# Separate instruction orders, a diagonal skip product and an own bank for the output product in the last 24 steps of a fused Mamba-style block and FP4 feed-forward

## Chip, core and metric

The kernel runs on one core of a Trainium2 chip. The metric is the device time of one execution in microseconds, the median of several runs.

## What is computed

The reference is one layer: a simplified state-space block and a feed-forward with blockwise FP4 rounding, each followed by a residual sum and layer norm. x is 8 x 2048 x 256 float32.

```python
xz = x @ W_in;  x_proj, z = split(xz)                  # 256 -> 2 x 512
x_conv = silu(causal_conv4(x_proj) + conv_b)
ssm = x_conv @ W_xproj                                 # 33 columns: delta, B (16), C (16)
delta = softplus(ssm[..., 0])
h_mean = einsum('bld,bln->bdn', x_conv, delta[..., None] * Bm) / L
y = einsum('bdn,bln->bld', h_mean, Cm)
y = (y + D * x_conv) * silu(z)
x1 = layernorm(x + y @ W_out)
gate, up = fp4_linear(x1, w_gate), fp4_linear(x1, w_up)   # 256 -> 704
out = layernorm(x1 + fp4_linear(silu(gate) * up, w_down)) # 704 -> 256
```

fp4_linear rounds both operands in groups of 16 along the contraction: absolute maximum, scale, division, rounding to the grid, product with the scale.

## The kernel before

Rows of x are worked in 32 groups of 512 rows (NSUP = 32), each group in four steps (j = 0 to 3), so a step is a quarter group. The first half, phase 1, makes x_conv and silu(z) of a group, writes both to HBM, and adds the group's share to the state h_mean, which is whole only when all four groups of a batch are through. The second half, phase 2, runs LAG = 5 groups later: it reads x_conv and silu(z) back (xl and zl, in the tile early), makes y, the output product, layer norm and the feed-forward for 128 rows per step. The loop `walk` therefore goes over g_ = 0 to 38. Each step works on seven different tiles at once, at different stages: u and v (phase 1), w (y, skip, gate), to (output product, attention sum, layer norm), tx (rounding of x), tg (gate and up product, rounding of h), td (down product), tz (FFN sum, second layer norm). Phase 1 ends with g_ = 31; its last pieces lie in g_ = 32. So for g_ = 33 to 38, the last 24 steps, only the later stages are left: y, skip and gate in the first 16 of them, everything but these in the next four, and the drain in the last four.

The order of work is written out by hand on each engine, as the body of `walk`, and semaphores tie them together. Each engine runs its queue in order, so that a wait holds everything behind it. In a late step:

- PE (TensorE): gate and up product into pgu (L518, 18 matmuls), six transposes of h into pe_ and pb (L558), y product into pc (L569, 48 rows deep, 512 columns), output product into pd (L580, four full-precision matmuls of 256 columns), two transposes of x into pe_ (L630), down product into pd (L518, 17 matmuls). Output and down product share the bank pd: down waits for the attention sum of the same step to have read it (r_done), the output product for the FFN sum (r2_done). State products (L591, 512 columns, full precision) belong to phase 1.
- DVE (VectorE): FFN sum (L1089), absmax (L908), scale (L911), inverse (L914), divide (L918, here "codes") and the two rounding steps (L924, L927) of x; h product (L1114); skip, xl times D plus pc, into g (L1033); absmax of h (L908), two subtractions that make the low parts of the transposed h, "rests" (L1123, L1126), h scale and inverse (L911, L914), attention sum (L1140), h codes (L918), rests of x (L1152), the two rounding steps of h (L924, L927). The scaled values are written before rounding; ScalarE makes 2^22 times their magnitude in between (L841 for x, L879 for h), and rounding waits for it.
- ACT (ScalarE): squared deviations (L755), magnitude of x (L841), SiLU of the gate (L845), high parts of the transposed h (L853, L856), output rows (L864), high part of the transposed x (L873), magnitude of h (L879), rows of the first layer norm (L890).
- POOL (GpSimd): layer norms (L404, L406, L408, one element a partition), product of x with its scale (L429), gate: g times zl (L446), product of h with its scale (L456, L458).
- SP (SyncE): all transfers, in the same step order: next xres, next xl and zl (after g_ready), the store of the finished tile (after out_ready).

## Time and profile before

| what | value |
|---|---|
| median of 3 runs | 2015.34 us (2013.84 to 2023.07) |
| profiled execution, its own time | 2014.19 us |
| its span, first to last instruction | 2012.3 us |
| PE busy | 1920.6 us, 95% |
| DVE busy | 1708.1 us, 85% |
| ACT busy | 1280.9 us, 64% |
| POOL busy | 1081.0 us, 54% |
| mean granted TensorE clock | 0.981 of full speed |
| chain that ended last | PE 83%, DVE 7%, issue 5%, ACT 3%, POOL 2% |

Busy time of an engine is the union of its instructions. The granted clock is a share of 2.4 GHz; 0.5 would be 1.2 GHz throughout. Starts are microseconds from the first instruction. A matmul's end is modelled, so times of TensorE are best read from one start to the next; the same holds for VectorE, where an instruction's row overlaps the next by a little. A full-precision matmul is written in two records.

### The profile page before, as it was taken

The page shows a single profiled execution, that of the slowest core. Times are in us where ns is not written, and L with a number is a line of the kernel's source. Part 1 is how long each engine was busy: PE and PEld are TensorE (multiplying, and loading weights), DVE is VectorE, ACT ScalarE, POOL GpSimd, SP SyncE. Part 2 cuts the span into 40 slices and gives each one's busy share as a digit, 9 for nine tenths or more (in the row PEclk, how much of TensorE's full clock was granted, in tenths as well). Part 3 has the DMA queues.
Part 4 walks back from the last instruction along what each step waited for, and adds up shares of the span by engine and source line. Part 5 has one row for each costly group of instructions (what it writes and reads, how often), then busy time and mean ns, then how long its engine had stood idle before and what let it go on. Part 6 is the DMA issues. An engine that isn't in the chain of part 4 may idle for free.

```text
span 2012.3 us, 33985 instructions
## 1 busy us (share of the span) xinstructions
PE 1920.6 (95%) x10148; PEld 1541.0 (77%) x10148; DVE 1708.1 (85%) x3293; ACT 1280.9 (64%) x2613; POOL 1081.0 (54%) x1774
## 2 busy tenths in 40 slices
PE   6898999999999999999999999999999999888886
PEld 5666788888888888878887888888887887666665
DVE  6655889988988898999888989988889898887886
ACT  6776666666766666666666666766666675444443
POOL 3534555555555555555555555555555555544543
PEclk8898999999999999999999999999999999989999
DMA  5234232323232232323232232323222322221200
GB/s 169 91 127 141 90 105 98 102 91 110 97 104 99 94 106 87 108 98 108 98 104 99 85 105 98 112 93 108 97 91 102 106 89 85 64 63 64 63 24 14
DMA packets 120307, 190.58 MB, mean 95 GB/s; under 512 B 15040, under 2 KB 49728, under 8 KB 120128
## 3 DMA queue, kind: packets, MB, share of 16 engines
q1 hardware_dynamic: 120128, 188.42, 28.0%
q8 instruction: 85, 1.39, 0.3%
q14 instruction: 94, 0.77, 0.1%
HBM read 104.48 MB, written 83.89 MB: 94 GB/s over the span
## 4 chain that ended last, share of the span: by engine, by line
PE 83%; DVE 7%; issue 5%; ACT 3%; POOL 2%; SPq 0%; DMA 0%; POOLq 0%; DVEq 0%; ACTq 0%
PE pgu L518 23%; PE pd L518 13%; PE pd L580 10%; PE pb L518 8%; PE pa L518 8%; PE pc L591 5%; PE pc L607 5%; PE pa L620 2%; PE pe_ L558 2%; PE pc L569 2%; PE pe_ L630 1%; DVE acc L1009 1%; PE pb L558 1%; DVE qsh L908 1%; DVE g L1033 1%
## 5 line engine op out<-in xcount | busy, mean ns | idle before, releaser
L518 PE MATMUL pgu<-wgu_hi,xqT 128*128 128x512 f32 (+1 forms) x1536 | 428.4, 387 | 1.0 <-ACT xqT L873 1.0
L518 PE MATMUL pd<-wd_hi,hqT 128*128 128x256 f32 (+1 forms) x1536 | 323.0, 302 | 21.7 <-DVE scratch L1140 17.4
L518 PEld LDWEIGHTS pgu<-wgu_hi,xqT 128*128 128x128 f32 x1536 | 279.3, 190 | 65.1 <-issue 2.0
L518 PEld LDWEIGHTS pd<-wd_hi,hqT 128*128 128x128 f32 (+1 forms) x1536 | 253.6, 195 | 49.9 <-issue 30.1
L580 PE MATMUL pd<-wout,g 128*128 128x256 f32 x1024 | 254.8, 392 | 0.0
L404 POOL TENSOR_SCALAR rs<-ssq 128x1 f32<-128x1 f32 x256 | 51.1, 200 | 379.0 <-issue 364.2
L924 DVE SCALAR_TENSOR_TENSOR scratch<-scratch 128x256 f32<-128x256 f32 (+2 forms) x258 | 171.2, 664 | 71.4 <-ACT scratch L879 57.9
L518 PE MATMUL pgu<-wgu_lo,xqT 128*128 128x512 f32 (+1 forms) x768 | 227.2, 377 | 0.0
L755 ACT ACTIVATE scratch<-scratch,sum 128x256 f32<-128x256 f32 x256 | 129.9, 507 | 152.6 <-DVE scratch L1089 134.7
L1009 DVE SCALAR_TENSOR_TENSOR acc<-xps,cw,acc 128x512 f32<-128x512 f32 x256 | 202.2, 790 | 28.7 <-POOL acc L438 24.0
L580 PEld LDWEIGHTS pd<-wout,g 128*128 128x128 f32 x1024 | 184.0, 189 | 49.7 <-issue 29.8
L446 POOL TENSOR_TENSOR g<-g,early 128x512 f32<-128x512 f32 x128 | 163.6, 1278 | 48.6 <-DVE g L1033 48.3
L458 POOL TENSOR_TENSOR scratch<-hnq,qsh 128x704 f32<-128x704 bf16 x128 | 188.8, 1475 | 0.0
L518 PE MATMUL pd<-wd_lo,hqT 128*128 128x256 f32 x640 | 184.9, 289 | 0.0
L408 POOL TENSOR_SCALAR nm<-sum,rs 128x1 f32<-128x1 f32 x256 | 152.5, 596 | 44.0 <-POOL rs L406 44.0
L438 POOL TENSOR_TENSOR acc<-acc,tap 128x512 f32<-128x512 f32 x128 | 164.2, 1283 | 11.4 <-ACT tap L799 11.4
L406 POOL TENSOR_TENSOR rs<-rs,nhalf 128x1 f32<-128x1 f32 x256 | 151.7, 592 | 21.6
L607 PEld LDWEIGHTS pc<-wxp,xcs 128*128 128x128 f32 x1024 | 134.1, 194 | 37.6 <-ACT xcs L782 20.6
L518 PEld LDWEIGHTS pgu<-wgu_lo,xqT 128*128 128x128 f32 x768 | 144.4, 190 | 23.3
L429 POOL TENSOR_TENSOR scratch<-xnq,qsx 128x256 f32<-128x256 bf16 x128 | 81.3, 635 | 130.2 <-DVE xnq L927 129.7
L607 PE MATMUL pc<-wxp,xcs 128*128 128x33 f32 x1024 | 128.3, 270 | 23.6 <-ACT xcs L782 16.5
L873 ACT ACTIVATE xqT<-pe_ 128x256 fp32r<-128x256 f32 x128 | 48.7, 381 | 152.7 <-PE pe_ L630 152.7
(130 smaller groups left out, 4542.9 us busy)
## 6 DMA issues: line engine op xcount, KB each, us to landing
sz_hbm<-szs SPq DMA_DIRECT2D x128, 256.0 KB, 2.0
xc_hbm<-xcs SPq DMA_DIRECT2D x128, 256.0 KB, 2.0
early<-xc_hbm SPq DMA_DIRECT2D x128, 256.0 KB, 2.7
early<-sz_hbm SPq DMA_DIRECT2D x128, 256.0 KB, 3.0
xin<-in_x_t_dram SPq DMA_DIRECT2D x32, 512.0 KB, 4.7
xres<-in_L_attn_x_dram SPq DMA_DIRECT2D x128, 128.0 KB, 2.4
out_dram<-scratch SPq DMA_DIRECT2D x128, 128.0 KB, 1.7
early<-in_L_attn_W_in_dram SPq DMA_DIRECT2D x2, 512.0 KB, 4.7
```

Of the source, the lines that this page charges most:

```text
L406: pool.tensor_tensor(rs[:, :], rs[:, :], nhalf[:, :], ALU.pow).then_inc(rs_done, 1)
L408: pool.tensor_scalar(nm[:, :], total[:, :], rs[:, :], -1.0 / DM, ALU.mult, ALU.mult)\
L438: pool.tensor_tensor(acc[:, j % 2, :], acc[:, j % 2, :], tap0[:, j % 2, :], ALU.add).then_inc(tap_done, 1)
L446: pool.tensor_tensor(g[:, second(s) % 2, j, :], g[:, second(s) % 2, j, :], zl[:, j % 2, :], ALU.mult).then_inc(g_ready, 1)
L458: pool.tensor_tensor(blocks(hq[:, 0:FF]), blocks(hnq[:, :]), spread(qsh[:, :, 1]), ALU.mult).then_inc(hprod_done, 1)
L518: mm = pe.matmul(bank, lhsT, rhs, start=(m == 0), stop=(m == len(pairs) - 1))
L580: mm = pe.matmul(pd[:, 0:DM], g[:, (second(s) + 1) % 2, c, j * P:(j + 1) * P], wout[:, c, :], start=(c == 0), stop=(c == NB - 1))
L591: mm = pe.matmul(pc[0:H3, :], dB[:, t, :], xct[:, (n - 1) % 2, t, :], start=(t == 0), stop=(t == TPS - 1))
L607: mm = pe.matmul(pc[:, t * NX:(t + 1) * NX], xcs[:, jb % 2, t * P:(t + 1) * P], wxp[:, jb, :], start=True, stop=True)
L755: act.activation(dev[:, :], r, ACT.Square, bias=total[:, :], scale=-1.0 * DM, accum_out=ssq[:, :]).then_inc(ssq_done, 1)
L924: return dve.scalar_tensor_tensor(v, big, HALF_STEP, v, ALU.max, ALU.add)
L1009: dve.scalar_tensor_tensor(acc[:, jb % 2, :], xps[:, jb % 2, k:k + ST], cw[:, jb, k:k + 1], acc[:, jb % 2, :], ALU.mult, ALU.add).then_inc ...
```

## The change

It touches only steps with g_ > NSUP, the last 24, and the preparation of one table in the group before.

- Skip: where VectorE computed xl * D + pc, TensorE now adds diag(D) times xl into the bank pc behind the y product (`skip_product`). The four diagonal matrices, `diag`, are made by ScalarE in step j = 2 of g_ = 32.
- Gate: VectorE multiplies pc by zl straight into g (`gated`); POOL's gate is left out, and the y product waits for the gate of the tile before in place of the skip.
- Output product: it goes to the bank pa, free of phase 1 by then (`out_bank`). It waits for the attention sum of the tile before, and the down product for the FFN sum of the tile before, no longer for this step's attention sum.
- The two layer norms get a deviation buffer each (`dev`).
- Orders: each engine has its own list for these steps. The other added functions (ffn_sum, x_codes, h_product and so on) hold the old statements unchanged, so that both lists can call them.

```diff
+        diag = sb("diag", [P, NB, P])
...
-        dev = over_scratch(DM)
+        dev = over_scratch(2 * DM).rearrange("p (n d) -> p n d", n=2)
...
+        def out_bank(g_):
+            return pa if g_ > NSUP else pd
...
+                    def x_values():
+                        pool.wait_ge(xq_link, 6 * tx + 6)
+                        at_least(pool, xq_pe, tx)
+                        pool.tensor_tensor(blocks(xv[:, :]), blocks(xnq[:, :]), spread(qsx[:, :, 1]),
+                                           ALU.mult).then_inc(xprod_done, 1)
+                    if exists(tx) and g_ > NSUP:
+                        x_values()
                     if exists(tz):
                         layer_norm(tz, ssq2_done, out_ready, rs2_eps, rs2_done, nm2_done, sum2, ssq2, rs2, nm2)
...
+                    if exists(to) and g_ > NSUP:
+                        layer_norm(to, ssq1_done, r1_ready, rs1_eps, rs1_done, nm1_done, sum1, ssq1, rs1, nm1)
+                    if p2 and g_ <= NSUP:
...
-                    if exists(to):
+                    if exists(to) and g_ <= NSUP:
...
-                wait_apart(pe, (h_ready, b - 1 if s == 0 else b), (ct_ready, g_ - LAG + 1), (yd_done, w),
+                wait_apart(pe, (h_ready, b - 1 if s == 0 else b), (ct_ready, g_ - LAG + 1), (g_ready if g_ > NSUP else yd_done, w),
                            (ssm_added, capped(v, NT)))
                 if j == 3 and g_ == LAG:
                     pe.wait_ge(h_added, g_)
-                pe.matmul(pc[:, :], hcat[:, j * P:(j + 1) * P], ctr[:, second(s), :], start=True, stop=True)\
-                    .then_inc(y_pe, 1)
-            def output_projection(j, s, i, tz):
+                mm = pe.matmul(pc[:, :], hcat[:, j * P:(j + 1) * P], ctr[:, second(s), :], start=True,
+                               stop=g_ <= NSUP)
+                if g_ <= NSUP:
+                    mm.then_inc(y_pe, 1)
+            def skip_product(j, i, w):
+                pe.wait_ge(xl_landed[j % 2], 16 * (2 * i + j // 2 + 1))
+                if w == 4 * (NSUP - LAG + 1):
+                    pe.wait_ge(diag_ready, NB)
+                pe.matmul(pc[:, :], diag[:, j, :], xl[:, j % 2, :], start=False, stop=True).then_inc(y_pe, 1)
+            def output_projection(j, s, i, g_, to, tz):
                 pe.wait_ge(g_ready, 4 * i)
-                at_least(pe, r2_done, capped(tz + 1, NT))
+                if g_ > NSUP:
+                    pe.wait_ge(ct_ready, NSUP)
+                    pe.wait_ge(r_done, to)
+                else:
+                    at_least(pe, r2_done, capped(tz + 1, NT))
+                bank = out_bank(g_)
                 if i == 1 and j == 0:
                     pe.wait_ge(w_landed, 32)
                     pe.wait_ge(ct_ready, LAG)
                 for c in range(NB):
-                    mm = pe.matmul(pd[:, 0:DM], g[:, (second(s) + 1) % 2, c, j * P:(j + 1) * P],
+                    mm = pe.matmul(bank[:, 0:DM], g[:, (second(s) + 1) % 2, c, j * P:(j + 1) * P],
                                    wout[:, c, :], start=(c == 0), stop=(c == NB - 1))
...
-            def down_projection(to, td):
+            def down_projection(g_, to, td):
                 pe.wait_ge(hqT_hi, 2 * td + 2)
                 pe.wait_ge(hqT_lo, 2 * td + 2)
-                pe.wait_ge(r_done, capped(to + 1, NT))
+                if g_ > NSUP:
+                    pe.wait_ge(r2_done, td)
+                else:
+                    pe.wait_ge(r_done, capped(to + 1, NT))
                 pairs = []
                 for c in range(FC):
                     pairs += [(hqT[:, c, :], wd_hi[:, c, :]),
...
+                    if g_ > NSUP:
+                        if exists(tg):
+                            gate_and_up(tg)
+                        if p2:
+                            y_product(j, s, b, g_, v, w)
+                        if exists(td):
+                            transposed_h(td, u)
+                        if exists(to):
+                            output_projection(j, s, i, g_, to, tz)
+                        if p2:
+                            skip_product(j, i, w)
+                        if exists(tx):
+                            transposed_x(td, tx)
+                        if exists(td):
+                            down_projection(g_, to, td)
+                        continue
...
-                act.activation(dev[:, :], r, ACT.Square, bias=total[:, :], scale=-1.0 * DM,
+                act.activation(dev[:, 0 if ssq is ssq1 else 1, :], r, ACT.Square, bias=total[:, :], scale=-1.0 * DM,
...
+                    if g_ > NSUP:
+                        if exists(tg):
+                            gate_silu()
+                        if exists(tx):
+                            x_big()
+                        if exists(td):
+                            h_highs()
+                        if exists(tz):
+                            deviations(r2_done, tz, r2[:, :], sum2, ssq2, ssq2_done)
+                        if exists(tx):
+                            x_highs()
+                        if exists(to):
+                            deviations(r_done, to, r1[:, j, :], sum1, ssq1, ssq1_done)
+                        if exists(tg):
+                            h_magnitude()
+                        if exists(to):
+                            r1_rows()
+                        if exists(tz):
+                            out_rows()
+                        continue
...
+                    if g_ == NSUP and j == 2:
+                        act.wait_ge(w_landed, 32)
+                        for c in range(NB):
+                            act.activation(diag[:, c, :], ident[:, :], ACT.Copy, scale=dsk[:, c:c + 1])\
+                                .then_inc(diag_ready, 1)
...
+                        dve.scalar_tensor_tensor(r1[:, j, :], out_bank(g_)[:, 0:DM], 1.0, xres[:, j % 2, :], ALU.mult, ALU.add,
+                                                 accum_out=sum1[:, :]).then_inc(r_done, 1)
...
+                    def gated():
+                        if w == 4 * (NSUP - LAG + 1):
+                            dve.wait_ge(g_ready, w)
+                        dve.wait_ge(y_pe, w + 1)
+                        dve.wait_ge(zl_landed[j % 2], 16 * (2 * i + j // 2 + 1))
+                        at_least(dve, o_pe, 4 * i - 4)
+                        dve.tensor_tensor(g[:, second(s) % 2, j, :], pc[:, :], zl[:, j % 2, :],
+                                          ALU.mult).then_inc(g_ready, 1)
+                    if g_ > NSUP:
+                        if exists(tz):
+                            ffn_sum()
+                        if exists(tx):
+                            x_codes()
+                        if exists(tg):
+                            h_product()
+                        if exists(tx):
+                            x_round()
+                        if exists(td):
+                            h_rests()
+                        if exists(tg):
+                            h_absmax()
+                        if exists(to):
+                            attn_sum()
+                        if exists(tg):
+                            h_scales()
+                            h_codes()
+                        if exists(tx):
+                            x_rests()
+                        if exists(tg):
+                            h_round()
+                        if p2:
+                            gated()
+                        continue
```

TensorE's queue, one step of the 16, from the end of the gate and up product to the start of the down product. Before:

```order
L518 MATMUL pgu<-wgu_hi,xqT 128x384 x2
L558 MATMUL pe_<-ident,scratch 128x128 x4
L558 MATMUL pb<-ident,scratch 128x128 x2
L569 MATMUL pc<-ctr,hcat 128x512
L580 MATMUL pd<-wout,g 128x256 x4
L630 MATMUL pe_<-ident,scratch 128x128 x2
L518 MATMUL pd<-wd_hi,hqT 128x256
```

After:

```order
L531 MATMUL pgu<-wgu_hi,xqT 128x384 x2
L582 MATMUL pc<-ctr,hcat 128x512
L571 MATMUL pe_<-ident,scratch 128x128 x4
L571 MATMUL pb<-ident,scratch 128x128 x2
L607 MATMUL pa<-wout,g 128x256 x4
L592 MATMUL pc<-early,diag 128x512
L657 MATMUL pe_<-ident,scratch 128x128 x2
L531 MATMUL pd<-wd_hi,hqT 128x256
```

The y product has moved ahead of the transposes, the output product writes pa, and a 512-column product of early (xl) and diag stands between it and the transposes of x.

VectorE's queue, one step of the 16, from the rounding of x and the h product on. Before:

```order
L924 SCALAR_TENSOR_TENSOR scratch<-scratch 128x256
L927 SCALAR_TENSOR_TENSOR xnq<-scratch 128x256
L1114 TENSOR_TENSOR scratch<-scratch,pgu 128x704
L1033 SCALAR_TENSOR_TENSOR g<-early,dsk,pc 128x512
L908 TENSOR_REDUCE qsh<-scratch 128x44
L1123 TENSOR_TENSOR hqT<-pe_,hqT 128x512
L1126 TENSOR_TENSOR hqT<-pb,hqT 128x256
L911 TENSOR_SCALAR qsh<-qsh 128x44
L914 RECIPROCAL qsh<-qsh 128x44
L1140 SCALAR_TENSOR_TENSOR scratch,sum1<-pd,xres 128x256
L918 SCALAR_TENSOR_TENSOR scratch<-scratch,qsh 128x704
```

After:

```order
L1187 TENSOR_TENSOR scratch<-scratch,pgu 128x704
L1016 SCALAR_TENSOR_TENSOR scratch<-scratch 128x256
L1019 SCALAR_TENSOR_TENSOR xnq<-scratch 128x256
L1196 TENSOR_TENSOR hqT<-pe_,hqT 128x512
L1199 TENSOR_TENSOR hqT<-pb,hqT 128x256
L1000 TENSOR_REDUCE qsh<-scratch 128x44
L1215 SCALAR_TENSOR_TENSOR scratch,sum1<-pa,xres 128x256
L1003 TENSOR_SCALAR qsh<-qsh 128x44
L1006 RECIPROCAL qsh<-qsh 128x44
L1010 SCALAR_TENSOR_TENSOR scratch<-scratch,qsh 128x704
L1225 TENSOR_TENSOR xqT<-pe_,xqT 128x256
```

The rounding of x (its first step L924 before, L1016 after) has moved behind the h product, the rests before the absmax of h, the attention sum before the h scale, and the skip is gone from this place.

VectorE's queue at the seam of two such steps, from the x rests over the h rounding. Before:

```order
L1152 TENSOR_TENSOR xqT<-pe_,xqT 128x256
L924 SCALAR_TENSOR_TENSOR scratch<-scratch 128x704
L927 SCALAR_TENSOR_TENSOR hnq<-scratch 128x704
L1089 SCALAR_TENSOR_TENSOR scratch,sum2<-pd,scratch 128x256
L908 TENSOR_REDUCE qsx<-scratch 128x16
```

After:

```order
L1225 TENSOR_TENSOR xqT<-pe_,xqT 128x256
L1016 SCALAR_TENSOR_TENSOR scratch<-scratch 128x704
L1019 SCALAR_TENSOR_TENSOR hnq<-scratch 128x704
L1242 TENSOR_TENSOR g<-pc,early 128x512
L1161 SCALAR_TENSOR_TENSOR scratch,sum2<-pd,scratch 128x256
```

The gate, g from pc and early (zl), now stands between the last rounding of h and the FFN sum.

## Rows read from the trace of the kernel before

**Rows 1.** Stretches: us, busy (count) of PE PEld DVE ACT POOL, clock, DMA, GB/s

```profile
1731.23:1930.42 199.19, 171.33 (x834) 137.54 (x833) 162.59 (x341) 86.99 (x193) 100.68 (x162) 0.92 0.19 60
1930.42:1976.42 46.00, 38.93 (x206) 32.27 (x205) 37.02 (x79) 21.02 (x47) 19.40 (x36) 0.95 0.06 18
1856.83:1869.91 13.08, 11.40 (x53) 9.32 (x53) 11.09 (x23) 6.00 (x13) 6.78 (x13) 0.87 0.26 84
1894.55:1906.12 11.57, 9.89 (x53) 7.91 (x52) 10.15 (x22) 5.41 (x12) 6.22 (x11) 1.00 0.21 68
```

**Rows 2.** Timeline, one step at clock 1.00: start, us, engine, line, operation [idle before]

```profile
1895.49 0.42 DVE L1089 SCALAR_TENSOR_TENSOR scratch<-pd,scratch 128x256 f32<-128x256 f32 x1
...
1895.91 1.43 POOL L458 TENSOR_TENSOR scratch<-hnq,qsh 128x704 f32<-128x704 bf16 x1
...
1896.35 1.02 DVE L911 TENSOR_SCALAR qsx<-qsx 128x16 f32<-128x16 f32 x1
...
1897.76 0.42 DVE L918 SCALAR_TENSOR_TENSOR scratch<-scratch,qsx 128x256 f32<-128x256 f32 x1
...
1898.67 0.42 DVE L924 SCALAR_TENSOR_TENSOR scratch<-scratch 128x256 f32<-128x256 f32 x1 [0.48 <-ACT scratch L841]
1898.69 0.76 ACT L845 ACTIVATE scratch<-pgu 128x704 f32<-128x704 f32 x1
...
1899.48 0.89 DVE L1114 TENSOR_TENSOR scratch<-scratch,pgu 128x704 f32<-128x704 f32 x1
...
1900.29 0.74 DVE L1033 SCALAR_TENSOR_TENSOR g<-early,dsk,pc 128x512 f32<-128x512 f32 x1
...
1900.95 0.88 DVE L908 TENSOR_REDUCE qsh<-scratch 128x44 f32<-128x704 f32 x1
...
1901.74 0.68 DVE L1123 TENSOR_TENSOR hqT<-pe_,hqT 128x512 fp32r<-128x512 f32 x1
...
1902.57 0.41 PE L630 MATMUL pe_<-ident,scratch 128*128 128x128 f32 x2 [0.90 <-DVE hqT L1123]
1902.67 0.18 DVE L911 TENSOR_SCALAR qsh<-qsh 128x44 f32<-128x44 f32 x1
...
1903.52 0.88 DVE L918 SCALAR_TENSOR_TENSOR scratch<-scratch,qsh 128x704 f32<-128x704 f32 x1
...
1903.75 0.36 PE L518 MATMUL pd<-wd_hi,hqT 128*128 128x256 f32 x1 [0.77 <-DVE scratch L1140]
...
1904.33 0.42 DVE L1152 TENSOR_TENSOR xqT<-pe_,xqT 128x256 fp32r<-128x256 f32 x1
...
1905.27 0.89 DVE L924 SCALAR_TENSOR_TENSOR scratch<-scratch 128x704 f32<-128x704 f32 x1 [0.52 <-ACT scratch L879]
...
1907.07 0.42 DVE L1089 SCALAR_TENSOR_TENSOR scratch<-pd,scratch 128x256 f32<-128x256 f32 x1
```

**Rows 3.** Timeline of TensorE alone, a phase 1 and 2 step without idle time

```profile
1592.27 0.73 PE L518 MATMUL pgu<-wgu_hi,xqT 128*128 128x512 f32 x2
...
1596.22 0.62 PE L518 MATMUL pa<-xt_hi,win_hi 128*128 128x512 f32 x2
...
1597.61 0.60 PE L558 MATMUL pe_<-ident,scratch 128*128 128x128 f32 x4
...
1598.78 1.99 PE L580 MATMUL pd<-wout,g 128*128 128x256 f32 x8
1600.70 3.63 PE L591 MATMUL pc<-xct,dB 128*48 128x512 f32 x8
1604.27 0.44 PE L630 MATMUL pe_<-ident,scratch 128*128 128x128 f32 x2
1604.46 0.71 PE L518 MATMUL pb<-xt_hi,win_hi 128*128 128x512 f32 x2
...
1607.13 0.37 PE L518 MATMUL pd<-wd_hi,hqT 128*128 128x256 f32 x1
...
1609.52 0.73 PE L518 MATMUL pgu<-wgu_hi,xqT 128*128 128x512 f32 x2
```

More of the change, by code:

```diff
@@ new lines, in x_highs, with h_magnitude @@
+                    def x_highs():
+                        act.wait_ge(xq_pe, tx + 1)
+                        act.activation(xqT[:, 0:KM, :], pe_[:, 0:DM].rearrange("p (c n) -> p c n", c=KM), ACT.Copy)\
+                            .then_inc(xqT_hi, 1)
+                    def h_magnitude():
+                        act.wait_ge(hq_link, 6 * tg + 4)
+                        act.activation(hbuf[:, 0:FF], hbuf[:, FF:2 * FF], ACT.Abs, scale=TWO22)\
+                            .then_inc(hbig_ready, 1)
@@ new lines, in r1_rows @@
+                    def r1_rows():
+                        act.wait_ge(nm1_done, to + 1)
+                        act.activation(r1[:, j, :], r1[:, j, :], ACT.Identity, bias=nm1[:, :], scale=rs1[:, :])\
+                            .then_inc(r1_ready, 1)
+                    if g_ > NSUP:
[18 more added lines that the diff above has]
+                        continue
@@ L877, in body @@
                     if exists(tg):
[L878 to L880 removed]
+                        h_magnitude()
                     if p1 and td >= 0:
@@ L1063, in mean_state, with ffn_sum, x_codes @@
                         dve.wait_ge(h_link, 2 * b)
+                    def ffn_sum():
+                        dve.wait_ge(dn_pe, tz + 1)
+                        at_least(dve, out_ready, tz)
+                        dve.scalar_tensor_tensor(r2[:, :], pd[:, 0:DM], 1.0, r1[:, j, :], ALU.mult, ALU.add,
+                                                 accum_out=sum2[:, :]).then_inc(r2_done, 1)
+                    def x_codes():
+                        x_ = r1[:, (j - 1) % TPS, :]
+                        wait_apart(dve, (r1_ready, tx + 1))
+                        q_absmax(x_, small_x).then_inc(xq_link, 1)
+                        at_least(dve, xprod_done, tx)
+                        dve.wait_ge(xq_link, 6 * tx + 1)
+                        q_scale(small_x).then_inc(xq_link, 1)
+                        dve.wait_ge(xq_link, 6 * tx + 2)
+                        q_inverse(small_x).then_inc(xq_link, 1)
+                        at_least(dve, xq_pe, tx)
+                        dve.wait_ge(xq_link, 6 * tx + 3)
+                        q_divide(x_, small_x, xv[:, :]).then_inc(xq_link, 1)
```

165 lines of the change are left out of this document (83 added, 82 removed).

## Prediction

> **What bounds the kernel now.** I read the page first (TensorE is busy nearly everywhere, so most of the program is bound by it), then the stretches that the change covers, then one step of them in order of time on all engines, and last a stretch in which TensorE never waits, for its prices.
>
> The changed steps begin with the gate product at 1731.23 us. Steps 1 to 16 of them (y product still alive) take 199.19 us, 12.45 each, and the next four 46.00 us, 11.50 each [rows 1]. The last four end at the span's end, 2012.3. TensorE is busy for 171.33 of the 199.19, so 14% of that stretch is lost to waiting; its granted clock is 0.92 there, and it is 1.00 in one step and 0.87 in another [rows 1]. A step at clock 1.00 takes 11.57 us, one at 0.87 takes 13.08 [rows 1]. So 12.45 consists of 11.57 of order and 0.88 of lower clock. The lower level (1.2 GHz in place of 2.4) comes after steps in which TensorE stood idle before the transposed x and again before the down product; in the step shown the idle time is 0.90 us on the transposed x and 0.77 on the first down matmul [rows 2].
>
> What makes 11.57? VectorE's own queue, read start to start [rows 2]. From the h product (1899.48): product 0.81, skip 0.66, absmax 0.79, both rests 0.93, scale, inverse and attention sum together 0.85, codes to first rounding 1.75 (this holds the x rests and the wait for ScalarE's magnitude), both roundings 1.80. Then, with the rows of the step's head (1895.49 on), FFN sum and x absmax 0.86, x scale and inverse 1.41, x divide to x rounding 0.91, x rounding 0.81. The sum is 11.58 against 11.57: VectorE has no free time except two waits for ScalarE of about 0.5 us. One of these pieces is strange: the x scale, 16 elements wide, takes 1.02 us, the h scale, 44 wide, takes 0.18. The long one ends at 1897.37, when POOL's 704-wide product ends (1895.91 + 1.43 = 1897.34) [rows 2]. It waited for POOL.
>
> **What TensorE costs when it never waits** [rows 3], start to start: gate and up 3.95, six transposes and the y product 1.17, output product 1.92, four state products of 512 columns in full precision 3.57, so 0.89 each, transposed x 0.19, down 2.39.
>
> **The change part by part.**
> 1. Skip product on TensorE, 16 of them. No row shows it. It moves 512 full-precision columns, as a state product does: 0.89. From below the bound is a cheaper kind of matmul: the y product also has 512 columns and is less than half of the 1.17, so 0.4 at most; from above it is twice a 256-column output matmul, 2 x 1.92/4 = 0.96. I take 0.89, since size and type are equal. A step on TensorE is then 3.95 + 1.17 + 1.92 + 0.89 + 0.19 + 2.39 = **10.51**.
> 2. Gate on VectorE in place of skip. A product of a PSUM and an SBUF operand of 512 columns is what the first rest is; both rests (768 columns) take 0.93, so 0.62. The old skip, also 512 from PSUM, takes 0.66. From above: POOL's price for a product, 1.43 us for 704 columns, gives 1.04. I take 0.66. POOL loses its gate, which no one then waits for; I count nothing.
> 3. VectorE's new order. Leaving out what is equal: the x rounding now stands behind the h product, and ScalarE does the magnitude of x behind the gate's SiLU. That wait is gone: divide to next is then some 0.36, as its own 256-wide work costs elsewhere in this queue (FFN sum and absmax, two such pieces, 0.86), not 0.91. The gate lies between the last h rounding and the FFN sum, so the x scale starts 0.66 later against POOL's product, and waits some 0.2 to 0.35 us, not 0.84. Loop: 0.81 + 0.81 + 0.93 + 0.79 + 0.85 + 1.75 + 1.80 + 0.66 + 0.86 + 0.92 (scale and inverse, 1.41 less 0.49) + 0.36 = **10.5**; 10.3 if the scale waits least. On the rule: the Trainium skill, "SBUF — State Buffer", section "Who interferes with whom", says that VectorE and GpSimd share one port pair as an exclusive lock, taken by an instruction with two SBUF inputs or in a two-port mode. The trace agrees in the 1.02 us row above. By that rule the gate, with one input in PSUM, is not held by POOL, but the h codes and first rounding can be, by the layer-norm chain: that is the second rival.
> 4. TensorE's new order and bank. The output product writes its own bank, so the down product no longer waits for this step's attention sum (0.77 us before it [rows 2]), and the transposed x stands behind output and skip product. Laid out from the gate product's start with the prices above: y 3.95, transposes 4.4, output 5.1, skip 7.0, transposed x 7.9, down 8.1, next gate 10.5. What they wait for: the h product starts 4.93 after the gate (1894.55 to 1899.48; SiLU from 1898.69 [rows 2]); x rounding 5.7 to 6.5; POOL's x product is a third of its 1.43, done by 7.2, before 7.9; rests done by 7.5; x rests at 4.93 + 0.81 + 0.81 + 0.93 + 0.79 + 0.85 + 0.81 + 0.42 = 10.35. The next gate product needs them, 0.16 before TensorE is free. h rounding ends at 12.7, POOL's product at 14.5, and the next step's transposes want it at 10.5 + 4.4 = 14.9. The y product waits for the gate of the step before, done at 13.4, and wants it at 14.5. Every wait is covered, by 0.15 to 1.1 us, so the period is TensorE's.
> 5. ScalarE moves its row outputs last, so SyncE stores a tile and sends the next loads later, but at the latest when the gate of the step before is done, 13.4 - 10.5 = 2.9 us into a step. The skip product needs them in the step after, over 8 us on. Nothing.
> 6. Four scaled copies (the diagonals) on ScalarE in the step group before. ScalarE is busy 86.99 of 199.19 us, 5.4 us a step; 704 columns cost it 0.76 [rows 1, 2], so four of 128 cost under 3 us, in a gap. Nothing, 1 to 3 us if the cover failed.
>
> With TensorE full, its clock should stay up: in the stretch of rows 3 steps of this kind follow each other without idle time. I add 0.1 us for small collisions: **10.6** a step. The next four steps have no y, skip and gate: TensorE needs 10.51 less 0.89 and 0.4, 9.2, but the next gate still waits for the x rests, 10.35; I take 10.45. The last four steps gain nothing: there the chain gate, SiLU, product, codes, POOL, transposes, down is the same in both orders.
>
> **Sum.** 16 x (12.45 - 10.6) = 29.6; 4 x (11.50 - 10.45) = 4.2; less 0.8 for the change of order. Gain 33. The profiled execution took 2014.19 us by its own time (span 2012.3), giving 1981.2; the median of the runs, 2015.34, lies 1.15 above it, giving **1982**. With the low price of the skip product and everything else ideal 10.35 a step, gain 38, 1977; with the high prices 11.0, gain 27, 1988.
>
> **The rivals.**
> A. The lower clock stays. Gaps of under 1 us were enough for it before [rows 2], and gaps of 0.2 could be too. TensorE is now the bound, so a clock of 0.92 costs 10.51/0.92 = 11.4 a step: 16 x 1.05 + 4 x 0.7 = 19.6, **1996**. Against it: rows 3 run closed up. The Trainium skill, "TensorE: Matmul & The Clock Gate", section "A second HAM failure mode: psum-queue depth-cycling", says that many micro-idles between groups of matmuls make the clock oscillate. The trace before agrees (0.87 to 1.00 by step). By that rule the closed-up order ends it, which is my forecast, and an imperfect one is this rival.
> B. VectorE becomes the bound through POOL. The layer norm of the attention tile now runs at the time of h codes and first rounding, both with two SBUF operands. Three small POOL pieces could hold VectorE as the x scale was held, 0.84 each time; with two such stalls and a slow gate (+0.4) the loop is 10.3 + 1.7 + 0.4, about 12.0: gain 7 to 10, **2006**, no change that can be told. For it: VectorE had only a sixth of a microsecond to spare in my layout. Against: POOL's layer norm works on one element per partition.
> C. Slower: TensorE gets 0.89 us more work a step and runs it at the lower level. Were the gaps kept and the waits behind skip product only moved, clock and work would multiply: 10.51/clock passes 12.95 (the old step plus its share of 10 us) at a clock of 0.81. At 0.75 a step is 14.0: 16 x 1.55 = 25 lost, **2040**. The trace has no whole step below 0.87 in this stretch, so this is unlikely.
>
> **Numbers.** 0.5% of this kernel, 10 us, is about what its measurement can tell from no change. Forecast 0.78, A 0.10, B 0.08, C 0.04. Faster takes forecast, A and a little of B: 0.89; same 0.07; slower 0.04. The range runs from the forecast's low end, with 1 us beyond, over rival A: 1976 to 1998.
>
> **What would show it.** Right: the 16 steps at 10.4 to 10.8 us, clock 1.00, TensorE closed up, skip product 0.89, gate on VectorE near 0.7 to 0.74 long, x scale at 0.4 to 0.6. Step 4 is wrong if the transposed x or the gate product waits for VectorE by more than 0.2. Rival A shows as clock under 0.97 with TensorE busy; B as h codes or rounding far over 0.89 with VectorE never idle; C as full-precision matmuls of twice their length. The prediction is wrong as a whole if the 16 steps take over 11.6 each.

## Result and profile after

| | before | after |
|---|---|---|
| median of the runs | 2014.59 us (2011.63 to 2023.07, 4 runs) | 1983.42 us (1983.16 to 1983.50, 4 runs) |
| span of the profiled execution | 2012.3 us | 1981.6 us |
| mean granted TensorE clock | 0.981 | 0.987 |
| ratio after to before, 95% interval | | 0.9843 [0.9826, 0.986] |

The change makes the kernel 31 us faster. The forecast was 1982, with a range of 1976 to 1998.

The page, busy time by engine and the clock in 40 slices:

```profile
PE 1916.1 (97%) x10180; PEld 1536.4 (78%) x10180; DVE 1700.7 (86%) x3293; ACT 1278.8 (65%) x2617; POOL 1071.9 (54%) x1758
...
PEclk8898999999999999999999999999999999999998
```

TensorE's share rises from 95 to 97%. These two lines hardly tell where the gain is; the stretches do. They answer to [rows 1]: the 16 steps, the next four, one of the 16, the next step, the rest. Columns: stretch, us, busy time (count) of PE, PEld, DVE, ACT, POOL, then granted clock, DMA share, GB/s.

```profile
1732.07:1901.81 169.74, 165.51 (x866) 132.42 (x865) 153.91 (x338) 83.78 (x191) 88.32 (x144) 1.00 0.22 69
1901.81:1944.21 42.40, 37.61 (x205) 30.59 (x205) 37.66 (x81) 21.18 (x49) 22.39 (x37) 1.00 0.08 23
1838.02:1848.62 10.60, 10.34 (x55) 8.27 (x55) 9.62 (x21) 5.30 (x13) 5.61 (x10) 1.00 0.22 75
1944.21:1955.16 10.95, 8.55 (x43) 6.97 (x43) 9.17 (x19) 5.19 (x12) 4.55 (x8) 0.90 0.04 12
1955.16:1981.60 26.44, 14.48 (x65) 12.18 (x64) 9.75 (x19) 6.82 (x16) 6.36 (x13) 0.69 0.06 20
```

The last two stretches, in the kernel before:

```profile
1976.42:1986.57 10.15, 7.42 (x44) 6.29 (x43) 8.66 (x19) 4.81 (x10) 3.50 (x7) 1.00 0.04 13
1986.57:2012.30 25.73, 12.57 (x65) 10.75 (x64) 9.71 (x19) 6.56 (x15) 6.37 (x13) 0.82 0.05 16
```

The account of the spans, 2012.3 - 1981.6 = 30.7, follows from them. The 16 steps went from 12.45 to 10.61 (199.19 - 169.74 = 29.45), the next four from 11.50 to 10.60 (3.60). The drain lost 0.80 and 0.71, together 1.5. The stretch begins 0.84 later than before; three kernels below whose programs up to there are equal to that of the change begin it at 1731.73, 1733.85 and 1731.93, so that this is within its scatter.

One step of after on all engines, to be held against [rows 2]: start, us, engine, line, operation, and in brackets the idle time before it with what ended it.

```profile
1838.02 0.70 PE L531 MATMUL pgu<-wgu_hi,xqT 128*128 128x512 f32 x2 [0.25 <-issue]
...
1840.27 0.68 DVE L1242 TENSOR_TENSOR g<-pc,early 128x512 f32<-128x512 f32 x1
...
1840.69 1.43 POOL L471 TENSOR_TENSOR scratch<-hnq,qsh 128x704 f32<-128x704 bf16 x1
...
1841.73 0.42 DVE L1003 TENSOR_SCALAR qsx<-qsx 128x16 f32<-128x16 f32 x1
1842.04 0.49 PE L582 MATMUL pc<-ctr,hcat 48*128 48x512 f32 x1
1842.14 0.76 ACT L871 ACTIVATE scratch<-pgu 128x704 f32<-128x704 f32 x1 [1.60 <-PE pgu L531]
...
1842.93 0.89 DVE L1187 TENSOR_TENSOR scratch<-scratch,pgu 128x704 f32<-128x704 f32 x1
...
1844.53 0.68 DVE L1196 TENSOR_TENSOR hqT<-pe_,hqT 128x512 fp32r<-128x512 f32 x1
...
1844.90 1.02 PE L592 MATMUL pc<-early,diag 128*128 128x512 f32 x2
...
1845.46 0.88 DVE L1000 TENSOR_REDUCE qsh<-scratch 128x44 f32<-128x704 f32 x1
...
1845.76 0.38 PE L657 MATMUL pe_<-ident,scratch 128*128 128x128 f32 x2
1845.90 0.37 PE L531 MATMUL pd<-wd_hi,hqT 128*128 128x256 f32 x1
...
1846.26 0.41 DVE L1215 SCALAR_TENSOR_TENSOR scratch<-pa,xres 128x256 f32<-128x256 f32 x1
...
1846.41 0.26 POOL L414 TENSOR_SCALAR nm<-sum,rs 128x1 f32<-128x1 f32 x1 [0.17 <-POOL rs L412]
...
1846.60 0.19 DVE L1003 TENSOR_SCALAR qsh<-qsh 128x44 f32<-128x44 f32 x1
...
1846.82 0.43 DVE L1006 RECIPROCAL qsh<-qsh 128x44 f32<-128x44 f32 x1
...
1847.29 0.89 DVE L1010 SCALAR_TENSOR_TENSOR scratch<-scratch,qsh 128x704 f32<-128x704 f32 x1
...
1848.10 0.42 DVE L1225 TENSOR_TENSOR xqT<-pe_,xqT 128x256 fp32r<-128x256 f32 x1
...
1848.62 0.71 PE L531 MATMUL pgu<-wgu_hi,xqT 128*128 128x512 f32 x2 [0.26 <-issue]
1849.03 0.97 POOL L414 TENSOR_SCALAR nm<-sum,rs 128x1 f32<-128x1 f32 x1 [0.17 <-POOL rs L412]
1849.04 0.92 DVE L1016 SCALAR_TENSOR_TENSOR scratch<-scratch 128x704 f32<-128x704 f32 x1 [0.52 <-ACT scratch L897]
```

Both old idle times of TensorE are gone: the transposed x (1845.76) and the down product (1845.90) start without waiting. The skip product takes 0.86 from start to next start. But TensorE is not full: it waits 0.26 in each step ahead of the gate product, which starts when the rests of x are done (1848.10 + 0.42 = 1848.52). So I formed **theory L**: a step is set by the loop gate product, SiLU, h product, then VectorE's queue down to the rests of x, next gate product. Its pieces, start to start: 4.12 to SiLU, 0.79, 0.81 h product, 0.79 x rounding, 0.93 h rests, 0.80 absmax, 0.34 attention sum, 0.22 scale, 0.47 inverse, 0.81 codes, 0.42 rests of x, 0.10 to TensorE: 10.60. VectorE's own loop, which goes over POOL's product that the x scale waits for (1840.69 + 1.43 = 1842.12, scale's end 1842.15), has no other wait than 0.52 for ScalarE, so it is as long. The next four steps, which have no y, skip and gate, also take 10.60, and there TensorE waits 0.52 ahead of the gate product (at 1933.60): the step gets no shorter although TensorE is busy 0.9 us less in it (9.40 against 10.34). The rival, **theory T**, is the prediction's: TensorE's queue sets the step, and the 0.26 is an artefact of modelled ends.

One more pair of rows stands there: POOL's 1-wide L414 takes 0.97 beside VectorE's first rounding (1849.03, 1849.04), both ending at 1850.0 within 0.04, and 0.26 at 1846.41. So it is POOL's layer norm that is held there and not VectorE's rounding, which takes 0.92.

### The profile page after: what moved, and what is told of

Same layout as the page of the kernel before. It is cut to its first block and busy times, and to the rows that moved or that the text cites. A ratio compares the mean times of both kernels' runs of the same rounds, so it can differ in the third digit from the quotient of the medians.

```text
span 1981.6 us, 34023 instructions
## 1 busy us (share of the span) xinstructions
PE 1916.1 (97%) x10180; PEld 1536.4 (78%) x10180; DVE 1700.7 (86%) x3293; ACT 1278.8 (65%) x2617; POOL 1071.9 (54%) x1758
## 5 line engine op out<-in xcount | busy, mean ns | idle before, releaser
L531 PE MATMUL pd<-wd_hi,hqT 128*128 128x256 f32 (+1 forms) x1536 | 314.9, 297 | 5.3 <-issue 2.1
L531 PEld LDWEIGHTS pd<-wd_hi,hqT 128*128 128x128 f32 (+1 forms) x1536 | 247.7, 191 | 28.6 <-issue 7.8
L410 POOL TENSOR_SCALAR rs<-ssq 128x1 f32<-128x1 f32 x256 | 61.5, 240 | 347.7 <-issue 335.1
L1016 DVE SCALAR_TENSOR_TENSOR scratch<-scratch 128x256 f32<-128x256 f32 (+2 forms) x258 | 171.6, 665 | 61.2 <-ACT scratch L897 57.9
L607 PE MATMUL pd<-wout,g 128*128 128x256 f32 x864 | 215.4, 392 | 0.0
L607 PEld LDWEIGHTS pd<-wout,g 128*128 128x128 f32 x864 | 155.4, 190 | 42.5 <-issue 25.8
L414 POOL TENSOR_SCALAR nm<-sum,rs 128x1 f32<-128x1 f32 x256 | 153.4, 599 | 43.8 <-POOL rs L412 43.8
L459 POOL TENSOR_TENSOR g<-g,early 128x512 f32<-128x512 f32 x112 | 143.1, 1277 | 24.0 <-DVE g L1125 23.8
L871 ACT ACTIVATE scratch<-pgu 128x704 f32<-128x704 f32 x128 | 96.4, 753 | 71.0 <-PE pgu L531 70.9
```

What stands on the lines that cost most here:

```text
L414: pool.tensor_scalar(nm[:, :], total[:, :], rs[:, :], -1.0 / DM, ALU.mult, ALU.mult)\
L459: pool.tensor_tensor(g[:, second(s) % 2, j, :], g[:, second(s) % 2, j, :], zl[:, j % 2, :], ALU.mult).then_inc(g_ready, 1)
L531: mm = pe.matmul(bank, lhsT, rhs, start=(m == 0), stop=(m == len(pairs) - 1))
L607: mm = pe.matmul(bank[:, 0:DM], g[:, (second(s) + 1) % 2, c, j * P:(j + 1) * P], wout[:, c, :], start=(c == 0), stop=(c == NB - 1))
L871: act.activation(hbuf[:, 0:FF], pgu[:, 0:FF], ACT.Silu).then_inc(sg_ready, 1)
L1016: return dve.scalar_tensor_tensor(v, big, HALF_STEP, v, ALU.max, ALU.add)
```

## Experiments

"Step" is the mean of the 16 steps, from gate product to gate product. Behind "Measured" stand the median of the runs with their range, and the ratio to the kernel before, run beside them, with its 95% interval.

**1. Attention sum moved behind h scale and inverse** (`e1_sum_in_shadow`)

```diff
                         if exists(tg):
                             h_absmax()
+                        if exists(tg):
+                            h_scales()
                         if exists(to):
                             attn_sum()
                         if exists(tg):
-                            h_scales()
                             h_codes()
```

> The changed kernel with one swap on VectorE in its last 24 steps: attention sum behind the h scale and inverse, not ahead of them, so that it runs while the codes wait for the inverse. Theory L (a loop from gate product over SiLU and VectorE's queue to the x rests and the next gate product sets 10.60 us a step): 0.18 us less a step, 10.42, 20 steps, about 1979.8 us. Theory T (TensorE's own work sets the step): no change, 1983.4.

Measured: 1984.75 (1983.68 to 1986.76), ratio 0.9852 [0.9838, 0.9867], step 10.63. No gain; theory L's number was missed. Why, stands in VectorE's timeline of this kernel:

```profile
1855.68 0.88 DVE L1000 TENSOR_REDUCE qsh<-scratch 128x44 f32<-128x704 f32 x1
1856.66 0.20 DVE L1003 TENSOR_SCALAR qsh<-qsh 128x44 f32<-128x44 f32 x1
1856.90 0.43 DVE L1006 RECIPROCAL qsh<-qsh 128x44 f32<-128x44 f32 x1
1857.24 0.36 DVE L1215 SCALAR_TENSOR_TENSOR scratch<-pa,xres 128x256 f32<-128x256 f32 x1
...
1857.53 0.88 DVE L1010 SCALAR_TENSOR_TENSOR scratch<-scratch,qsh 128x704 f32<-128x704 f32 x1
```

Absmax, scale, inverse and codes depend on each other, and an instruction that reads what the one before has just written starts later than an independent one. In after, an independent instruction stands between absmax and scale (0.80 to the next start) but none between inverse and codes (0.47). Here it is the other way round: 0.98 and, over the sum, 0.34 + 0.29. Absmax to codes takes 1.83 in after and 1.85 here. One latency stays open in either place, so the run decides nothing between L and T; it shows that the edit frees nothing.

**2. The skip product issued twice** (`e2_skip_twice`; the output counts the skip twice)

```diff
-                pe.matmul(pc[:, :], diag[:, j, :], xl[:, j % 2, :], start=False, stop=True).then_inc(y_pe, 1)
+                pe.matmul(pc[:, :], diag[:, j, :], xl[:, j % 2, :], start=False, stop=False)
+                pe.matmul(pc[:, :], diag[:, j, :], xl[:, j % 2, :], start=False, stop=True).then_inc(y_pe, 1)
```

> The changed kernel with the diagonal product issued twice (skip is counted twice in the output). Theory L: TensorE had 0.26 us of idle time a step, so a second product of 0.86 costs 0.60 in 16 steps, 11.20 a step, about 1993 us. Theory T: 0.86 each, 11.46 a step, 1997.

Measured: 1991.41 (1990.26 to 1993.22), ratio 0.9884 [0.9868, 0.9901], step 11.14. The 16 steps in this kernel:

```profile
1732.73:1910.97 178.24, 178.24 (x897) 138.28 (x896) 154.19 (x339) 81.61 (x191) 81.14 (x145) 1.00 0.21 66
```

TensorE is busy for all of it. 0.86 us of work more cost 0.53, so 0.33 a step had been free, and the step of 11.14 lies at the 11.20 that theory L gave and not at the 11.46 of theory T: theory L. TensorE's own queue with one skip product is 11.14 - 0.86 = 10.28.

**3. Absolute maximum of x in PSUM** (`e12_psum_alone`). The scale's input then lies in free columns of the bank pa.

```diff
                     pe.wait_ge(r_done, to)
+                    pe.wait_ge(xq_link, capped(6 * (to - 1) + 2, 6 * NT))
...
-            small_x = [qsx[:, :, r] for r in range(3)]
+            small_x_early = [qsx[:, :, r] for r in range(3)]
+            small_x_late = [pa[:, DM:DM + QX]] + small_x_early[1:]
...
+                        small_x = small_x_late if g_ > NSUP else small_x_early
...
```

> The change with only the absolute maximum of x in the PSUM bank pa. If POOL's product holds instructions with SBUF inputs, the x scale falls from 0.42 to about 0.18 us here. Theory L says that the loop over the gate product is a bound of its own: the step stays at 10.55 to 10.60, the time at 1983. If VectorE's own loop through POOL alone were the bound: 0.24 less a step, about 1979.

Measured: 1984.12 (1982.52 to 1985.57), ratio 0.9844 [0.9822, 0.9866], step 10.61. In its timeline:

```profile
1840.62 1.43 POOL L471 TENSOR_TENSOR scratch<-hnq,qsh 128x704 f32<-128x704 bf16 x1
...
1841.66 0.18 DVE L1004 TENSOR_SCALAR qsx<-pa 128x16 f32<-128x16 f32 x1
...
1842.86 0.89 DVE L1192 TENSOR_TENSOR scratch<-scratch,pgu 128x704 f32<-128x704 f32 x1 [0.20 <-ACT scratch L872]
```

Two findings. The scale takes 0.18, and begins and ends while POOL's product runs: it was this product that held it, and a PSUM input frees it. The freed 0.24 us turns into a wait of 0.20 for the SiLU in front of the h product: the loop over the gate product is 10.60 by itself.

**4. Gate and rests of x moved on VectorE** (`e11_order_alone`)

```diff
                         if exists(tg):
                             h_scales()
-                            h_codes()
                         if exists(tx):
                             x_rests()
                         if exists(tg):
-                            h_round()
+                            h_codes()
                         if p2:
                             gated()
+                        if exists(tg):
+                            h_round()
```

> The change with the order on VectorE alone (h scales, rests of x, h codes, gate, h rounding), absolute maximum of x in SBUF as before. The gate no longer stands between the h rounding and the FFN sum, so POOL's product, which starts when the h rounding ends, is later against the x scale. Theory L with the hold of the scale by POOL: the x scale takes 0.7 to 1.0 us in place of 0.42, a step 10.6 to 10.8, the time 1984 to 1987. If POOL doesn't hold the scale, this one is as fast as the kernel with both edits, about 1980.

Measured: 1986.31 (1985.62 to 1987.63), ratio 0.9856 [0.9834, 0.9878], step 10.66. In its timeline:

```profile
1843.48 1.42 POOL L471 TENSOR_TENSOR scratch<-hnq,qsh 128x704 f32<-128x704 bf16 x1
...
1844.30 0.64 DVE L1003 TENSOR_SCALAR qsx<-qsx 128x16 f32<-128x16 f32 x1
...
1844.95 0.66 PE L571 MATMUL pe_<-ident,scratch 128*128 128x128 f32 x4 [0.33 <-POOL scratch L471]
```

The gate now fills half of VectorE's wait for ScalarE (0.26 of 0.52 is left), and the rests of x stand ahead of the codes; but POOL's product comes later against the x scale, which it holds to its end (1843.48 + 1.42 = 1844.90, scale's end 1844.94). The transposes of h wait 0.33 for the same product.

**5. Both** (`e10_order_and_psum`): the edits of 3 and 4 together.

> The change with two edits for its 24 steps. Order on VectorE: h scales, rests of x, h codes, gate, h rounding (the gate fills the wait for ScalarE's magnitude, the rests of x stand ahead of the codes). And the absolute maximum of x goes into free columns of the PSUM bank pa, so that the x scale has no SBUF input that POOL's product could hold. Theory L (the 10.60 us of a step are the loop gate product, SiLU, VectorE's queue, rests of x, next gate product, and VectorE's own loop through POOL): both loops fall under TensorE's 10.3 to 10.35, a step takes about 10.4, the time is about 1979.6. Rival T (something else, such as TensorE's own queue, sets 10.60): 1983.4, no change.

Measured: **1977.90** (1976.57 to 1979.56), ratio 0.9814 [0.9792, 0.9836], step 10.39, the next four 10.19. The 16 steps, and two rows of one of them:

```profile
1731.73:1897.91 166.18, 165.35 (x866) 132.23 (x865) 149.98 (x339) 83.24 (x191) 90.27 (x143) 1.00 0.22 71
```

```profile
1839.30 0.18 DVE L1004 TENSOR_SCALAR qsx<-pa 128x16 f32<-128x16 f32 x1
...
1845.78 0.73 PE L531 MATMUL pgu<-wgu_hi,xqT 128*128 128x512 f32 x2
```

TensorE is busy 165.35 of 166.18, and the gate product no longer waits. Each edit alone gave nothing, both together 5.5 us beyond the change; the slowest execution, 1979.56, is faster than the fastest of either edit alone, 1982.52. Of the 6.7 us that the span is shorter, 5.2 lie in the twenty steps and 1.1 in the drain. There were two loops of equal length, and each edit shortened one. Now TensorE's queue sets the step, as the prediction had it for the change. This version beats both kernels.

**6. Old bank, new orders** (`e4_shared_bank`)

```diff
-            return pa if g_ > NSUP else pd
+            return pd
```

(with the old waits for r_done and r2_done).

> The changed kernel with output and down product in one bank again. Down must wait for this step's attention sum. Theory L: down starts 0.8 later, gate product at its end, 0.5 later: 11.1 a step over 20 steps, about 1993 us, clock 1.00 or a little under. If the bank matters little (the wait hides in the loop through VectorE): 1983 to 1985.

Measured: 1997.84 (1997.54 to 1999.79), ratio 0.9918 [0.9903, 0.9933], step 11.21, next four 11.58. The down product waits for the attention sum again, at clock 1.00:

```profile
1845.68 0.36 PE L531 MATMUL pd<-wd_hi,hqT 128*128 128x256 f32 x1 [0.68 <-DVE scratch L1208]
```

The bank is worth 0.60 a step inside the new orders, 0.98 in the next four (at clock 0.96 there). The step is near the expected 11.1; the time is 5 us above the expected 1993, in part for these four.

**7. Own bank alone, in the kernel before** (`e6_bank_alone`)

> The kernel before with only the own bank for the output product in the last 24 steps. VectorE's queue of 11.58 us still sets the step. With the clock as before 12.45 a step, 2014; with the clock up 11.6, 2001. If the bank alone brought the gain, 1985.

Measured: 2007.34 (2006.32 to 2010.38), ratio 0.9953 [0.9939, 0.9968], step 11.81, but single steps between 10.72 and 13.33, and the clock 0.95. None of the three expected times came. The wait for the attention sum ahead of the down product is gone, but TensorE arrives earlier at the transposed x and waits there for VectorE's rests of h, 1.80 in the steps of 11.57 and in one of 13.33 even longer:

```profile
1837.74 0.41 PE L639 MATMUL pe_<-ident,scratch 128*128 128x128 f32 x2 [2.15 <-DVE hqT L1135]
```

**8. Diagonal product and gate on VectorE alone, in the kernel before** (`e5_diagonal_alone`): old orders and old bank, the skip product behind the y product, the gate where the skip had been.

> Old lists and old bank, but skip as diagonal product (right behind y) and gate on VectorE in the place of the skip. VectorE waits about 0.4 longer for pc and saves 0.06: about 12.0 us a step at clock 1.00, since TensorE is fuller; about 2007 us. If the clock falls as before, 12.8 a step, 2020. If the diagonal product alone brought the gain, 1985.

Measured: 2011.90 (2011.22 to 2013.54), ratio 0.998 [0.9969, 0.9991], step 12.10, clock 1.00. At the place of the old skip:

```profile
1845.78 1.12 PE L588 MATMUL pc<-early,diag 128*128 128x512 f32 x2
...
1846.94 0.69 DVE L1197 TENSOR_TENSOR g<-pc,early 128x512 f32<-128x512 f32 x1 [0.45 <-PE pc L588]
```

VectorE now waits 0.45 for TensorE's extra work. The order at clock 1.00 gets longer by about that (11.57 to 12.07 in the steady steps), the lower clock goes away, and 0.35 a step is left. The step came as expected (12.0), the time not (2007): the next four steps take 46.96 at clock 0.93 and the drain is 1.3 longer than before.

**9. Change without the diagonal product** (`e3_skip_back_on_vector`): skip on VectorE behind the x rounding, gate on POOL; new orders and bank kept.

> The changed kernel without the diagonal product: skip on VectorE behind the x rounding, gate on GpSimd, as before; new orders and own bank kept. Theory L: skip lies in the loop, 0.66 more, 11.26 a step at clock 1.00, about 1994 us. If TensorE, idle 16% of the time again, also loses its clock as before (0.92): up to 12.1 a step, about 2007.

Measured: 2003.00 (2000.55 to 2004.51), ratio 0.9925 [0.9909, 0.9942], step 11.80. Its 16 steps, then what POOL's gate does in one, and TensorE's idle times in the next:

```profile
1734.65:1923.48 188.83, 156.47 (x833) 125.20 (x833) 172.78 (x339) 82.28 (x191) 91.93 (x161) 1.00 0.20 62
```

```profile
1837.85 1.29 POOL L457 TENSOR_TENSOR g<-g,early 128x512 f32<-128x512 f32 x1
...
1838.47 0.72 DVE L998 TENSOR_SCALAR qsh<-qsh 128x44 f32<-128x44 f32 x1
...
1841.02 0.70 PE L529 MATMUL pgu<-wgu_hi,xqT 128*128 128x512 f32 x2 [1.04 <-issue]
...
1849.02 0.41 PE L654 MATMUL pe_<-ident,scratch 128*128 128x128 f32 x2 [0.96 <-DVE hqT L1191]
```

The diagonal product with the gate on VectorE is worth 1.19 a step in the new order: 0.66 for the skip, which here lies in the loop over the gate product (between h product and rests), while the gate of the change lies outside it, and 0.53 for POOL's gate, which holds the h scale (the gate ends at 1839.14, the scale at 1839.19). 10.60 + 0.66 + 0.53 is 11.79, and the steady steps take 11.77 to 11.80. The hold by POOL was not foreseen: neither 11.26 nor the fall of the clock came. TensorE's 0.86 us of work less bring nothing.

**10. A filler in the kernel before** (`e7_filler_in_before`, 512 columns; `e13_small_filler`, 256 columns): a useless full-precision product into the free bank pa, behind each output product of the late steps. The last four steps have none, so it runs in 20 steps. The edit shown is the large one; the small one writes pa[:, 0:DM] from columns 0:DM.

```diff
+                    if g_ > NSUP and exists(to):
+                        if g_ == NSUP + 1 and j == 0:
+                            pe.wait_ge(ct_ready, NSUP)
+                        pe.matmul(pa[:, :], wout[:, 0, 0:P], g[:, (second(s) + 1) % 2, j, :], start=True, stop=True)
```

> The kernel before with one useless full-precision product of 512 columns (0.89 us) behind each output product of the last 24 steps, into a free bank, where TensorE idled 0.9 us. If 0.88 us a step was lost to the lower clock through idle time: clock 1.00, 11.6 a step, 14 us faster than before, about 2000. If the clock does not hang on that idle time or the filler only adds work: 2014 or more, up to 2028.

> The kernel before with a useless full-precision product of 256 columns in each of the 24 steps behind the output product, half of the filler that gave 2001.4. If the granted clock follows TensorE's idle time in proportion, it lies between 0.92 and 1.00 (about 0.96 to 0.97), the step at 11.6 to 12.1 and the time at 2002 to 2009. If the half is enough to hold the clock at 1.00: 11.6 a step or less, about 2000. If the clock has nothing to do with the idle time (the larger filler helped in another way): no change, 2014.

Measured: 2001.36 (2000.25 to 2003.89), ratio 0.9923 [0.9908, 0.9938] with the large one, 2003.54 (2001.48 to 2008.94), ratio 0.9953 [0.9934, 0.9972] with the small one. The 16 steps of the first and of the second:

```profile
1732.40:1919.12 186.72, 172.17 (x866) 132.74 (x865) 163.34 (x340) 86.29 (x192) 100.47 (x161) 1.00 0.21 64
```

```profile
1731.94:1918.60 186.66, 165.27 (x865) 132.75 (x864) 163.26 (x340) 86.32 (x192) 100.47 (x161) 1.00 0.20 64
```

```profile
1845.54 0.41 PE L630 MATMUL pe_<-ident,scratch 128*128 128x128 f32 x2 [0.48 <-DVE hqT L1127]
...
1846.72 0.36 PE L518 MATMUL pd<-wd_hi,hqT 128*128 128x256 f32 x1 [0.78 <-DVE scratch L1144]
```

The last two rows are one step of the small filler. Work that nobody needs makes the kernel before 13 and 11 us faster, and it adds only to TensorE's queue: the step falls from 12.45 to 11.67. The steady steps take 11.58, as the step at clock 1.00 in [rows 1] did. So 0.78 of each step was lower clock, and filling TensorE's idle time gives it back. The other 0.10 of the 0.88 is order: most of it is the first of the 16 steps, which takes 12.55 at clock 1.00 before and 12.54 with the large filler. In the profiled execution of the small filler the clock does not follow the idle time in proportion: with 0.48 + 0.78 of idle time a step it is 1.00, with 0.90 + 0.77 [rows 2] it is 0.92 on the mean. The timed runs leave that open: their median, 2003.54, lies in the 2002 to 2009 that a clock in proportion would give, and in the one of 2008.94 the clock of the whole execution is 0.983 in place of 0.987 to 0.990.

**11. Old orders for the drain** (`e8_old_drain`): the new lists hold for 20 steps, the last four use the old ones.

```diff
-                    if g_ > NSUP:
+                    if NSUP < g_ < NSUP + LAG + 1:
```

> The changed kernel with the old lists in the last four steps only (g_ = 38). The drain grew by 1.5 us, since the x rounding behind the h product lets TensorE idle 2.3 us before the transposed x and its clock falls. If so, 1.5 us less, about 1981.9; if the drain's growth has another cause, 1983.4.

Measured: 1984.91 (1984.12 to 1985.71), ratio 0.9852 [0.9837, 0.9867]. The rest, from 1956.33 on, is as short as in the kernel before (25.69), but the step before it takes 12.66. The expectation fell. The first row is of the change, the second of this kernel, at the same place:

```profile
1951.56 0.44 PE L657 MATMUL pe_<-ident,scratch 128*128 128x128 f32 x2 [2.33 <-POOL scratch L426]
```

```profile
1952.46 0.66 PE L657 MATMUL pe_<-ident,scratch 128*128 128x128 f32 x2 [3.75 <-DVE hqT L1196]
```

At the seam VectorE runs behind TensorE, and TensorE stands idle there with either list. In the version of experiment 5 the same step takes 10.24 at clock 1.00 and the rest 26.01, so its two edits win back 1.1 of the 1.5 us.

## Why the prediction was right, point by point

- **What bounds the kernel, and the 0.88 of lower clock.** Right in kind, and shown by experiment 10; the size is 0.78, and 0.10 more is order. The change has the 16 steps at clock 1.00, as forecast; rival A did not come.
- **Item 1, skip product 0.89.** Right: 0.86. The sum of 10.51 for TensorE was somewhat high; its own queue is 10.28 by experiment 2 and 10.39 by experiment 5, mostly since the output product takes 1.73 (1843.17 to 1844.90 in the change) and not 1.92.
- **Item 2, gate 0.66.** Right for VectorE: 0.60 to the next start, row 0.68. "POOL loses its gate, which no one then waits for; I count nothing" was wrong: in the new order POOL's gate would hold the h scale for 0.53 of each step (experiment 9). I did not look for what the removed instruction would collide with in the new order. The number did not suffer, since the forecast was laid out without that collision.
- **Item 3.** The x scale waits 0.24, forecast 0.2 to 0.35. The rule quoted there, from the Trainium skill, "SBUF — State Buffer", section "Who interferes with whom", agrees with experiments 3, 4 and 9: scales with both sides in SBUF end with POOL's product, the one that reads PSUM takes 0.18 beside it. Mis-sized was "scale, inverse and attention sum together 0.85": in the new order they take 1.03, because nothing stands between inverse and codes any more. The divide was put at "some 0.36" from two pieces that take 0.86 together, which is 0.43 each; it took 0.38.
- **Item 4 is the step that failed.** It said "Every wait is covered, by 0.15 to 1.1 us, so the period is TensorE's". The rests of x were to be done at 10.35 and TensorE free at 10.51. They are done at 10.50 (0.18 more by the term above, 0.03 less by the others), 0.10 passes before TensorE starts, and TensorE would be free at 10.34. So a wait of 0.26 sets the step, by a loop over SiLU and VectorE, and a second loop over POOL is as long. That 10.6 came out nevertheless is luck in part: 10.51 plus 0.1 for collisions, where it was 10.34 plus 0.26. It matters for what one would try next: with TensorE as the bound, the edits of experiment 5, which touch VectorE's queue alone, could have gained nothing, and they gained 5.5 us.
- **The next four steps**, forecast 10.45, measured 10.60: the same mis-sized term. The hand-over of 0.10 stands where 0.1 for collisions had been added. 0.6 us in all.
- **The drain "gains nothing".** It lost 1.5 us. In the last-but-one of the stretches TensorE waits 2.33 for POOL's product of x, and the down product behind it and part of the next gate product run at the lower clock (0.90 and 0.69 of the stretches, against 1.00 and 0.82). That the old order was no cure is experiment 11. With the two edits of experiment 5 the drain is 36.25, against 37.39 in the change and 35.88 before; what the best order there is, was not tried.
- **Items 5 and 6** cost nothing that a row shows.
- **Sum.** Forecast 29.6 + 4.2 - 0.8 = 33; measured 29.45 + 3.60 - 0.84 - 1.5 = 30.7. The median stands 1.4 above the forecast.
- **Rivals B and C** did not come: VectorE is held by POOL once a step only, for 0.24. Where POOL's layer norm meets codes and rounding, it is POOL that is held (0.97 against 0.26), so the two further stalls of 0.84 did not come. Rival B's sum was also wrong: 10.3 + 1.7 + 0.4 is 12.4 and not 12.0, which would have left a gain of about 1 in the 16 steps.

The parts do not add. Diagonal alone gives 0.35 a step, bank alone 0.64, all together 1.84. Taken out of the finished change, the bank costs 0.60, about what it brings alone, and the diagonal product 1.19, over three times what it brings alone. So the diagonal product counts only in the new surroundings. Whether these are the orders or the bank is not shown: the new orders alone, and both parts together in the old orders, were not run.

## What to carry to other kernels

Lay out the step as loops (from one instruction round to the same one in the next step) with every hand-over between engines in it, and compare all loops that come within a few tenths: where two are equal, an edit that shortens one alone shows nothing, and both together pay, as in experiments 3 to 5. Small VectorE instructions with operands in SBUF are worth looking up by their own duration: the x scale that read 1.02 before and 0.42 in the change was waiting for GpSimd, and with its input in PSUM it took 0.18 (experiment 3). Moving work onto TensorE can pay twice where TensorE has gaps, by the work and by the clock; a filler product tells which.

## What the hardware showed that I had not expected

- The clock does not follow TensorE's busy share. In experiment 9 TensorE is busy for 83% of the 16 steps, with idle times of 1.04 and 0.96 us, at clock 1.00; before, it is 86% at 0.92 [rows 1], with gaps of 0.90 and 0.77 [rows 2]; experiment 7 has 87% at 0.95. The Trainium skill, "TensorE: Matmul & The Clock Gate", section "A second HAM failure mode: psum-queue depth-cycling", lays the oscillation, in another kernel, to many micro-idles between groups of matmuls. Experiment 10 agrees with that; experiment 9 has such gaps and no oscillation, so the idle time alone does not decide it here. What tells them apart stays open. In the kernel before, the steps at clock 0.87 and at 1.00 show the same two waits (0.91 and 0.78, 0.90 and 0.77).
- A useless product of half the length was enough for clock 1.00 in the profiled execution.
- An instruction on VectorE that depends on the one before starts some 0.1 to 0.2 us later than an independent one: inverse to codes takes 0.47, inverse to the independent attention sum 0.34; absmax to scale takes 0.98, absmax to the sum 0.80 (experiment 1).
